# Context and half of Wk loaded ahead of Wq, and the keys multiplied ahead of the average of Wq

## What is computed

```python
def xattn(x, y, Wq, bq, Wk, bk, Wv, bv, Wo, bo):      # x is normalised
    q, k, v = heads(x @ Wq + bq), heads(y @ Wk + bk), heads(y @ Wv + bv)
    weights = softmax(einsum('bhqd,bhkd->bhqk', q, k) / sqrt(32))
    return merge(einsum('bhqk,bhkd->bhqd', weights, v)) @ Wo + bo

x = x + tanh(g_xattn) * xattn(layernorm(x), ctx, Wq, bq, Wk, bk, Wv, bv, Wo, bo)
x = x + tanh(g_ffn) * quantised_linear(layernorm(x))   # int8 rows, int8 weights, scale, bias
```

## Time and profile before

| | us |
|---|---|
| median of 3 runs | 813.43 (812.89 to 814.37) |
| the profiled execution | 812.92 |
| its span, first to last instruction | 811.0 |
| TensorE busy | 791.6 |
| VectorE, ScalarE, GpSimd busy | 575.5, 555.6, 517.4 |

### The profile page before, as it was taken

How to read it: one execution, slowest core, us unless ns; L and a number is a source line. 1 busy time by engine, 2 the same in 40 slices (tenths; PEclk the granted TensorE clock), 3 DMA queues, 4 the chain that set the end, 5 groups by cost and what they waited for, 6 DMA issues and landing times.

```text
span 811.0 us, 17119 instructions
## 1 busy us (share of the span) xinstructions
PE 791.6 (98%) x6629; PEld 521.2 (64%) x6658; DVE 575.5 (71%) x916; ACT 555.6 (69%) x845; POOL 517.4 (64%) x518
## 2 busy tenths in 40 slices
PE   8899999999999999999999999999999999999995
PEld 6665667666666666666666666667667666666563
DVE  4878677686767767677586757867678575767668
ACT  5676587676776767676676775767677666777685
POOL 4626484765758566594765758567494765756587
PEclk9999999999999999999999999999999999999998
DMA  8531605142241422315232151422314131111112
GB/s 292 217 83 75 201 28 163 60 144 71 66 132 53 162 79 59 112 53 167 74 117 74 48 172 53 144 79 66 123 54 143 66 92 54 40 53 53 53 52 104
DMA packets 39631, 79.68 MB, mean 98 GB/s; under 512 B 6912, under 2 KB 8320, under 8 KB 37504
## 3 DMA queue, kind: packets, MB, share of 16 engines
q1 hardware_dynamic: 38976, 77.75, 29.8%
q10 hardware_dynamic: 576, 0.85, 0.3%
HBM read 61.78 MB, written 16.81 MB: 97 GB/s over the span
## 4 chain that ended last, share of the span: by engine, by line
PE 89%; DVE 3%; issue 3%; POOL 2%; ACT 1%; DMA 1%; SPq 0%; DVEq 0%; ACTq 0%; POOLq 0%
PE bank_a L340 25%; PE bank_b L340 24%; PE scores L395 8%; PE sum_ps L424 7%; PE scores L412 7%; PE pv_ps L428 6%; PE bank_a L472 3%; PE scores L415 2%; PE pv_ps L472 2%; PE bank_b L472 1%; DVE row_max L1092 1%; PE bank_b L447 1%; PE sum_ps L403 1%; PE bank_a L447 1%; DMA wk_stage<-in_wk 1%
## 5 line engine op out<-in xcount | busy, mean ns | idle before, releaser
L1092 DVE TENSOR_REDUCE row_max<-scores 128x16 f32<-128x1920 f32 x64 | 138.1, 2158 | 109.0 <-PE scores L395 109.0
L773 ACT ACTIVATE probs<-scores 120x2048 f32<-120x2048 f32 x64 | 120.4, 1882 | 77.3 <-PE scores L415 77.2
L1445 POOL TENSOR_TENSOR x<-x,u_sb 128x512 f32<-128x512 f32 x56 | 75.8, 1353 | 127.3 <-DVE u_sb L1181 125.0
L1440 POOL TENSOR_TENSOR x<-x,gbias_r 128x512 f32<-128x512 f32 x64 | 83.0, 1297 | 44.0 <-ACT cen L797 44.0
L395 PEld LDWEIGHTS scores<-k_sb,q_sb 32*128 32x128 f32 x2048 | 63.0, 186 | 53.0 <-issue 41.6
L1432 POOL TENSOR_TENSOR o_lo<-on,o_hi 128x512 fp32r<-128x512 f32 x48 | 62.7, 1307 | 51.7 <-ACT o_hi L791 51.0
L1398 POOL TENSOR_TENSOR xt<-xt,rstd_b 128x512 f32<-128x512 f32 x60 | 92.4, 1564 | 2.3 <-ACT rstd_b L1026 2.3
L1428 POOL TENSOR_TENSOR x<-x,gbo_r 128x512 f32<-128x512 f32 x64 | 88.6, 1396 | 2.4 <-DMA x<-in_x 2.3
L395 PE MATMUL scores<-k_sb,q_sb 32*128 32x120 f32 x2048 | 74.7, 282 | 1.3 <-issue 1.0
L424 PE MATMUL sum_ps<-probs,ones_f 120*32 120x512 f32 x512 | 68.2, 605 | 0.2 <-ACT probs L773 0.2
L428 PE MATMUL pv_ps<-probs,v_sb 120*32 120x512 f32 x512 | 66.6, 592 | 0.0
(11 more groups left out here) (225 smaller groups left out, 2000.4 us busy)
## 6 DMA issues: line engine op xcount, KB each, us to landing
xt<-in_x_t SPq DMA_DIRECT2D x16, 1024.0 KB, 5.6
x<-in_x SPq DMA_DIRECT2D x64, 256.0 KB, 3.0
out_x<-x SPq DMA_DIRECT2D x61, 256.0 KB, 2.1
x_in<-in_x SPq DMA_DIRECT2D x60, 256.0 KB, 3.0
rstd_b<-rstd_rows SPq DMA_DIRECT2D x14, 256.0 KB, 4.7
ctx_sb<-in_ctx_t SPq DMA_DIRECT2D x8, 360.0 KB, 4.8
probs<-in_wq SPq DMA_DIRECT2D x4, 256.0 KB, 3.5
x<-in_wo SPq DMA_DIRECT2D x1, 1024.0 KB, 9.6
```

The source lines that it names most:

```text
L773: act.activation(probs[0:KEYS], scores[0:KEYS], ACT.Exp, scale=SCALE).then_inc(p_ready, 1)
L1092: dve.tensor_reduce(row_max[:].rearrange("p (t r) j -> p r t j", r=ROWG)[:, :, :, j], scores[:, :, 0:QT * KEYS].rearrange("p r (t k) -> p ...
L1440: pool.tensor_tensor(x1_of(m)[:, t], x1_of(m)[:, t], gbias_r[:], ALU.add).then_inc(x1b_ready, 1)
L1445: pool.tensor_tensor(x1_of(m)[:, t], x1_of(m)[:, t], u_sb[:], ALU.add).then_inc(out_ready, 1)
```

## The change

The transfers of context and of the first half of Wk are issued first, then the first quarter of Wq, the second half of Wk and the other three quarters of Wq. TensorE follows: key groups 0 and 1, the first quarter of the average, key groups 2 and 3, the other three quarters. The average's sum, its bank and its signal stay as they are. No other engine's code is touched.

```diff
--- before.py
+++ after.py
@@ -246,11 +246,12 @@
                 sp.wait_ge(out_ready, nth(n, QT, t))
                 sp.dma_start(out_v[n, t], x1_of(n)[:, t]).then_inc(out_stored[n % 2][t], 16)
 
-            for c in range(DT):
-                load(wq_landed[c], wq_stage[:, c], rows(wq)[:, c])
             load_ctx(0)
             load(wk_landed[0], wk_stage[:, :, 0:D // 2], rows(wk)[:, :, 0:D // 2])
+            load(wq_landed[0], wq_stage[:, 0], rows(wq)[:, 0])
             load(wk_landed[1], wk_stage[:, :, D // 2:D], rows(wk)[:, :, D // 2:D])
+            for c in range(1, DT):
+                load(wq_landed[c], wq_stage[:, c], rows(wq)[:, c])
             load_xt(0)
             for t in range(QT):
                 load(x0_landed[t], x0_stage[t], x_v[0, t])
@@ -339,6 +340,13 @@
                 for p, (a, b) in enumerate(((0, 0), (0, 1), (1, 0))):
                     ins = pe.matmul(out_ap, stat[a], mov[b], start=first and p == 0, stop=last and p == PASSES - 1)
                 return ins
+
+            def mean_wq(chunks):
+                for c in chunks:
+                    pe.wait_ge(wq_landed[c], 16)
+                    ins = pe.matmul(pv_ps[:], mean_of, wq_stage[:, c], start=c == 0, stop=c == DT - 1)
+                    if c == DT - 1:
+                        ins.then_inc(wq_mean, 1)
 
             def keep_running(count, bank):
                 for _ in range(count):
@@ -669,12 +677,12 @@
             first, second = range(DT // 2), range(DT // 2, DT)
             pe.wait_ge(consts_ready, 5)
             keep_running(5, pv_ps)
-            for c in range(DT):
-                pe.wait_ge(wq_landed[c], 16)
-                ins = pe.matmul(pv_ps[:], mean_of, wq_stage[:, c], start=c == 0, stop=c == DT - 1)
-            ins.then_inc(wq_mean, 1)
-            for j in range(DT):
-                project_k_whole(j, scores[:, j])
+            project_k_whole(0, scores[:, 0])
+            project_k_whole(1, scores[:, 1])
+            mean_wq(range(1))
+            project_k_whole(2, scores[:, 2])
+            project_k_whole(3, scores[:, 3])
+            mean_wq(range(1, DT))
             project_q_whole(0, bank_a)
             project_q(0, 1, bank_b, first)
             pe.wait_ge(ident_ready, 1)
```

## The result

| us | before | changed |
|---|---|---|
| median | 813.21 (812.89 to 814.37, 4 runs) | 820.04 (820.00 to 820.28, 4 runs) |
| ratio | 1 | 1.0086, 95% interval 1.0071 to 1.0101 |
| the profiled execution | 812.92 | 820.28 |
| its span | 811.0 | 818.4 |

The change costs 6.8 us, where 3.9 had been forecast (817.3) and the range ended at 819.3. The kernel is slower, as expected, by more than expected. In the profiled executions the difference is 7.4 us.

A forecast was written before the change was run, and what follows sets the result against it. The prediction took the chain behind the average of Wq, ending 6.15 us later, to set the start: after slack, +4.0 us at the first scores, less 0.1 given back, +3.9, median 817.3 us; range 815.0 to 819.3.

The forecast's parts named there:

- The landing: Start of the kernel: context and the first half of Wk, loaded first, are usable by TensorE at 5.55 us.
- the order: TensorE's start: keys ahead of most of the average, so the average ends at 14.09 instead of 7.94, 6.15 us later.
- the slack: Waits behind the average that absorb delay: VectorE 2.57 us, ScalarE 1.31 and 0.60, GpSimd 1.95.
- 14.13 for centring: VectorE's centring of Wq, behind the average, runs from 14.13 to 16.61 us; before, it started at 7.98.
- the +4.0 taken: Delay of the first scores, before at 21.65 us, chosen from engine delays of +3.85, +3.95 and +4.2; bounds +3.1 and +5.5.
- The chain of waits, read alone: Start of the kernel: its chain names Wk's landing at 8.87 us, so bringing Wk earlier would move all forward.
- rival 4: Key multiplies set the start and centring has slack, so earlier Wk brings all forward by 3.4 us: 810.0; chance 0.04.
- The port collision: VectorE's `xt_lo` meets GpSimd's fourth `wq_lo` on the shared SBUF port: 0.7 us on VectorE, just hidden behind the copy.
- key groups 0 and 1 are half of the 24 records, 2.55 us: TensorE's first key multiplies after the change: they run from 5.55 to 8.10 us.
- the rivals (1): First two key groups start at a slower clock after TensorE's idle 4.18 to 5.55: +1.3 us, 818.6; chance 0.13.
- The gap of 1.06 us at 7.94: TensorE's wait for Wk before the change left keys at 0.21 us; used as argument against a slower clock.
- 2 us of idle time behind the first query group: TensorE, ending the first query group at 18.3, waits for the first `xt_lo` at 20.5 before query group 1.

The follow-up runs named there:

- experiment 5: Changed kernel with ten instead of five warm-up matmuls, whole average between key groups 1 and 2, second half of Wk loaded last: median 815.01 us.
- experiment 1: Changed kernel with ten instead of five warm-up matmuls on constants: median 817.66 us against 812.94 before; two of six executions at 821.3.
- 2: Changed kernel with ten warm-up matmuls and twelve matmuls on constants between the first query group and query group 1: median 818.71 us.
- 7: Changed kernel with ten warm-up matmuls and six matmuls on constants ahead of the first turn of the maxima: median 818.12 us, five executions.
- 3: Loads in the change's order, TensorE's order as before (average first, then all keys): median 817.26 us against 812.94 before.
- 6: Kernel before with one instead of five warm-up matmuls: median 813.61 us against 813.15, ratio 1.0005.
- 4: TensorE's order of the change, loads in the order of before: median 823.29 us, from 823.01 to 826.66.
- 8: Kernel before with the first half of query group 2 ahead of the first scores, the second half behind them: median 813.73 us against 813.15, ratio 1.0010.
- 9: Kernel before with three matmuls on constants ahead of the first turn of the maxima: median 812.93 us against 812.83, ratio 0.9998.

## Why the prediction was wrong

**The landing, the order and the slack were right.** Data was usable at 5.43 (5.55). The other twelve key records took 2.59 (2.55). The average is what the start hangs on: experiment 5 moves it with the work unchanged, and the time follows. Without any loss to the clock the piece is 11.55 us, so the forecast's 14.13 for centring gives 25.7 for the first scores (forecast: 25.55 by its rows, 25.65 by the +4.0 taken) and 25.7 + 791.1 = 816.8 us, which is the forecast for the profiled execution. The chain of waits, read alone, would have had the kernel faster (rival 4); in the table the average's end decides. Of the three engines, ScalarE and GpSimd came out as argued. The port collision too: the four `xt_lo` took 3.22 us instead of 2.46, 0.76 more, where 0.7 had been taken, and the statistic behind them was hidden ahead of the copy as said.

**The step that failed is "key groups 0 and 1 are half of the 24 records, 2.55 us".** They took 5.14: every record ran at half the rate. It stood among the rivals (1), with a chance of 0.13 and a price of +1.3 us; the price was 2.6. Two arguments were wrong there. The gap of 1.06 us at 7.94 in the kernel before came after TensorE had reached full rate, and says nothing about one that comes before it has. The changed kernel went from its warm-up, all at half rate, into a wait of 1.26 us, and stayed at half rate for the next 5 us. And the price assumed that the clock would rise halfway, for which no row spoke. Experiments 1, 2, 5 and 7, which keep TensorE occupied until the keys, bring them to 2.60 to 3.28 us. The Trainium skill (TensorE: Matmul & The Clock Gate, "What's actually happening") has half rate as the default that activity releases; the 0.85 us spacing in experiments 3 and 6 agrees, and 5.14 against 2.59 us puts this kernel among them.

**A second loss was not foreseen at all.** The sum names 2 us of idle time behind the first query group and books nothing for it. It was 2.57 us, and from 24 to 28 us the granted clock read 0.56 and 0.59. The turn of rstd, due at 25.05 when `ln_rstd` was done, started at 25.82 and took 1.05 us instead of 0.60. By the table it cost 12.61 - 11.55 = 1.06 us.

Together: 3.9 forecast, + 2.41 for centring at 16.54 instead of 14.13, + 1.06 for the second loss = 7.4 us, which is the difference of the profiled executions (820.28 - 812.92 = 7.36). The medians differ by 6.8, as the profiled execution of before lies 0.3 us under its median and that of the changed kernel 0.2 above.

What stays open is when this second drop comes. Four profiles have the wait of 2.56 or 2.57 us ahead of query group 1. In the changed kernel and in 4 and 7 the clock drops behind it, in 1 it doesn't, though 1 and 7 run the same program up to there. So it differs between executions. The drop was seen and priced; its condition wasn't settled. Nor does any run hold the wait ahead of the keys apart from the length of the warm-up.

## What to carry to other kernels

The end of the chain of waits names what was awaited last, not what it costs to be late elsewhere: before moving a step later, follow who waits for its result on each engine and subtract the idle time found there; here 8.56 us later in the average became 7.4 us in the end. A step put first to use early data is only early if TensorE arrives at it in full clock: a short warm-up followed by a wait bought nothing, and idle time that the change creates has to be priced at the clock too. Where executions of one kernel fall in two groups, profile one of each: a 0.23 us operation that took 1.61 cost 3.3 us with the slow clock behind it.

## What the runs showed that was not expected

- The granted clock reads 1.00 in the first 10 us of the changed kernel, while its records run at half rate. At the start the durations tell the rate (0.43 against 0.21 us per key record), the clock column doesn't; later it does (0.50, with durations doubled).
- A wait of 2.0 us was followed by up to 7 us at 0.50 (experiments 1, 4 and 8 had it). Beyond the hold itself (792.30 in the table) that cost 2.2 us in 1 and 4 and 0.4 in 8. It starts only after TensorE is at work again: 42 to 44 us, when it idles, still read 1.00.
- A VectorE subtraction on 64 numbers per partition took 1.61, 1.60, 1.63 and 1.58 us (experiments 1, 4, 7, 8) beside GpSimd's scaling of x, and 0.22 to 0.25 otherwise. The Trainium skill (SBUF — State Buffer, "SBUF: two separate sides") has one of the two engines block fully until the other's operation is done, when VectorE reads two SBUF inputs and GpSimd reads SBUF. These rows agree: one GpSimd operation there takes 1.5 us, and the held subtraction of experiment 1 ends 0.09 us behind it.
- The same start reached full rate at 4.7, about 6.5 and about 7.2 us (the kernel before, experiments 8 and 9), while the first scores of before and of 9 started within 0.2 us of each other: the slack hid it. One profile of a start is one draw.
